# State-space section of a small vision network: a quarter of the products made with time along partitions, C spread by DMA, chunks ordered by state group first

## What is computed

```python
def _mamba(x, Win, convw, convb, Wx, Wdt, bdt, Alog, Dp, Wout):   # D_INNER 512, D_STATE 32, DT_RANK 16, D_CONV 4
    u, z = jnp.split(jnp.einsum('bld,ed->ble', x, Win), 2, axis=-1)
    ...                                                            # causal convolution of u over 4 taps
    uc = _silu(uc)
    x_dbl = jnp.einsum('bld,ed->ble', uc, Wx)
    dt = jax.nn.softplus(jnp.einsum('blr,dr->bld', x_dbl[..., :DT_RANK], Wdt) + bdt)
    Bv, Cv = x_dbl[..., DT_RANK:DT_RANK + D_STATE], x_dbl[..., DT_RANK + D_STATE:]
    A = -jnp.exp(Alog)
    def step(h, ins):
        dt_t, B_t, C_t, u_t = ins
        h = jnp.exp(dt_t[..., None] * A) * h + (dt_t * u_t)[..., None] * B_t[:, None, :]
        return h, jnp.einsum('bdn,bn->bd', h, C_t)
    ...
    y = ys.transpose(1, 0, 2) + uc * Dp
    return jnp.einsum('bld,ed->ble', y * _silu(z), Wout)
```

## Time and profile before

| | |
|---|---|
| median of 3 runs | 3977.64 us (3972.79 to 3995.63) |
| the profiled execution | 3975.0 us |
| its span, first to last instruction | 3973.3 us |
| mean granted TensorE clock | 0.942 |
| TensorE matmuls busy | 3398.2 us (86%) |
| VectorE busy | 2701.4 us (68%) |
| ScalarE busy | 2065.3 us (52%) |
| GpSimd busy | 1935.7 us (49%) |

### The profile page before, as it was taken

One profiled execution on the slowest core, in us unless ns is written; L12 is line 12 of the kernel. 1 busy time (PEld: TensorE's weight loads), 2 busy tenths in 40 slices (PEclk: granted clock), 3 DMA queues, 4 the chain that ended last, 5 costly groups with the idle time before them and its releaser, 6 DMA issues. The chain is left out here.

```text
span 3973.3 us, 59932 instructions
## 1 busy us (share of the span) xinstructions
PE 3398.2 (86%) x18880; PEld 2341.8 (59%) x18880; DVE 2701.4 (68%) x4104; ACT 2065.3 (52%) x4736; POOL 1935.7 (49%) x1912
## 2 busy tenths in 40 slices
PE   1869989989996888898888888998887889999868
PEld 0646666667654566666666666666655655555544
DVE  6442255643236999999999999999997444444441
ACT  0332223332227777787778777877774244444422
POOL 0123200000315998999999999899985000000035
PEclk9989999999997999999999999999999999989865
DMA  3068610002950000000000000000000000000035
GB/s 97 2 224 316 247 62 1 1 18 107 312 198 28 1 1 2 1 1 2 1 14 1 4 1 2 1 1 2 1 1 11 26 1 1 1 1 1 3 113 170
DMA packets 66606, 196.70 MB, mean 50 GB/s; under 512 B 12609, under 2 KB 37177, under 8 KB 55769
## 3 DMA queue, kind: packets, MB, share of 16 engines
q1 hardware_dynamic: 54936, 161.60, 11.9%
q0 software_dynamic: 11328, 30.95, 2.4%
HBM read 166.53 MB, written 25.99 MB: 48 GB/s over the span
## 5 line engine op out<-in xcount | busy, mean ns | idle before, releaser
L1905 DVE TENSOR_TENSOR_SCAN ssm_hs<-ssm_da,ssm_pb 128x512 f32<-128x512 f32 x1024 | 1236.3, 1207 | 3.6 <-ACT ssm_da L1744 3.6
L1444 POOL TENSOR_TENSOR ssm_hc<-ssm_hs,ssm_cb 128x1024 f32<-128x1024 f32 x512 | 1207.6, 2359 | 0.0
L1541 PE MATMUL ssm_py<-ssm_hc,ident 128*128 128x256 f32 x4096 | 1061.4, 382 | 2.8 <-POOL ssm_hc L1444 2.6
L1744 ACT ACTIVATE ssm_da<-ssm_dt,ssm_an 128x255 f32<-128x255 f32 x2048 | 871.7, 502 | 133.4 <-POOL ssm_dtu L1392 89.9
L1541 PEld LDWEIGHTS ssm_py<-ssm_hc,ident 128*128 128x128 f32 x4096 | 705.6, 191 | 79.6 <-POOL ssm_hc L1444 5.7
L1888 DVE TENSOR_TENSOR ssm_pb<-ssm_pb,ssm_dtu 128x512 f32<-128x512 f32 x1024 | 690.5, 674 | 29.6 <-PE ssm_pb L1527 25.8
L1527 PE MATMUL ssm_pb<-ssm_bst,ssm_eyeb 96*128 96x256 bf16 x2048 | 403.7, 279 | 208.1 <-DVE ssm_hs L1905 192.8
L1527 PEld LDWEIGHTS ssm_pb<-ssm_bst,ssm_eyeb 96*128 96x128 bf16 x2048 | 147.5, 98 | 485.3 <-DVE ssm_hs L1905 410.1
L1134 DVE TENSOR_REDUCE duo_mxr<-duo_ring 128x4 f32<-128x1024 f32 x128 | 156.7, 1225 | 200.4 <-PE duo_ring L861 189.2
L2374 PE MATMUL moe_pu<-moe_up,moe_xt 128*128 128x512 f32 x568 | 269.8, 598 | 1.8 <-ACT moe_xt L2504 1.8
L2246 POOL DMA_INDIRECT moe_xr<-moe_x_dram,moe_rowx x71 | 68.9, 971 | 345.6 <-PE ln_ps L2363 197.7
(11 more groups left out here) (590 smaller groups left out, 5791.0 us busy)
## 6 DMA issues: line engine op xcount, KB each, us to landing
moe_up<-in_moe_up SPq DMA_DIRECT2D x72, 1024.0 KB, 7.4
moe_down<-in_moe_down SPq DMA_DIRECT2D x72, 512.0 KB, 4.9
sw_wt<-in_sw_w SPq DMA_DIRECT2D x47, 192.5 KB, 2.9
moe_x_dram<-moe_tok SPq DMA_DIRECT2D x32, 128.0 KB
moe_yg<-moe_y_dram SPq DMA_DIRECT2D x16, 256.0 KB, 3.1
tok_w<-in_wd SPq DMA_DIRECT2D x4, 576.0 KB, 13.4
out<-h SPq DMA_DIRECT2D x1, 2056.0 KB, 6.3
tok_pix<-in_img SPq DMA_DIRECT2D x1, 2048.0 KB, 9.7
```

Of the source, the lines that this page charges most:

```text
L1444: nc.gpsimd.tensor_tensor(hc[:, n % 2, part_], hs[:, n % 2, part_], cb[:, q * NQ_ + 4 * half:q * NQ_ + 4 * half + 4, :], ALU.mult).then_in ...
L1541: ins = nc.tensor.matmul(py[:, j % 2, 0:L], k.ident[:], hc[:, n % 2, st, :], start=False, stop=(q == QN - 1 and st == NQ_ - 1))
L1744: ins = nc.scalar.activation(da[:, n % 2, 2 * m + o, 1:L], dt2[:, v, j, 1:L], ACT.Exp, scale=a_n[:, d, j, st:st + 1])
L1905: nc.vector.tensor_tensor_scan(two(hs[:, n % 2, 2 * m:2 * m + 2, :]), two(da[:, n % 2, 2 * m:2 * m + 2, :]), two(pb[:, p % 4]), 0.0, ALU.m ...
```

## The change

- **Order of chunks:** the group of states q is outermost, the channel block j innermost. `cb` holds two groups of eight states instead of all 32; all four blocks' sums are open at once (`sums`), and `out_chunk` runs four times at the start of the next unit.
- **C by DMA:** `spread_c` and ScalarE's 32 copies go. ScalarE copies the rows of B and C to `crow`; SyncE stores C to DRAM (`store_c`) and loads one group, spread to all partitions, at a time (`load_c`), when GpSimd has finished the group that used the buffer.
- **The last two states of each chunk (step m = 3):** dt u is turned by TensorE to time along partitions (`turn_steps`, eight 128x128 transposes a unit) and copied by ScalarE (`take_steps`). There B of one state is a column, so ScalarE makes the product of all 512 channels with a scale (`products`, two passes of 512 columns per state and group). TensorE turns it back into `pb` (`turn_products`, four transposes in place of two matmuls), and VectorE makes only 48 products a unit in place of 64.
- **Directions:** `take` goes; `project` reads `x` itself and ScalarE reads the projections backwards.
- **Places:** the work for the next unit stands two to four chunks earlier; `last_token` and `lead` now stand after chunk 0, all of `soften` before the unit begins (chunks 11 and 12). The last states are copied once a chunk.
- **Waits:** VectorE waits for `hc` once a chunk, at step 0, for both halves of chunk n - 2.

```diff
-        cb = sb("cb", [P, NS_, L])
+        cb = sb("cb", [P, 2, NQ_, L])
...
+                def store_c(u, v):
+                    sp.wait_ge(s["crow_in"], u + 1)
+                    sp.dma_start(c_dram[bass.ds(u, 1)].rearrange("o n t -> (o n) t"), crow[NS_:2 * NS_, v, :]).then_inc(s["c_out"], 16)
+
+                def load_c(u, q):
+                    if q == 0:
+                        sp.wait_ge(s["c_out"], Turn(u, 16)(16))
+                    sp.wait_ge(s["hc_done"], Turn(u, 2 * NCH, 16)(2 * DJ * (q - 1)))
+                    sp.dma_start(cb[:, q % 2], c_dram[bass.ds(u, 1), q * NQ_:(q + 1) * NQ_, 0:L].rearrange("o n t -> (o n) t").partition_broadcast(P)).then_inc(s["c_odd" if q % 2 else "c_even"], 16)
...
                     for n in range(NCH):
-                        j, q = n // QN, n % QN
+                        q, j = n // DJ, n % DJ
                         if j == 0:
-                            pool.wait_ge(s["c_free"], c_free(NQ_ * (q + 1)))
+                            pool.wait_ge(s["c_odd" if q % 2 else "c_even"], Turn(u, 32)(16 * (q // 2 + 1)))
...
-                            nc.gpsimd.tensor_copy(h_l[:, v, j, q * NQ_ + 4 * half:q * NQ_ + 4 * half + 4], hs[:, n % 2, part_, L - 1])
-                            nc.gpsimd.tensor_tensor(hc[:, n % 2, part_], hs[:, n % 2, part_], cb[:, q * NQ_ + 4 * half:q * NQ_ + 4 * half + 4, :], ALU.mult).then_inc(s["hc_done"], 1)
-                        if before is not None:
+                            if half:
+                                nc.gpsimd.tensor_copy(h_l[:, v, j, q * NQ_:(q + 1) * NQ_], hs[:, n % 2, :, L - 1])
+                            nc.gpsimd.tensor_tensor(hc[:, n % 2, part_], hs[:, n % 2, part_], cb[:, q % 2, part_, :], ALU.mult).then_inc(s["hc_done"], 1)
+                        if n == 0 and before is not None:
+                            last_token(u - 1, 1 - v, before)
+                        if n == 12:
+                            last_rate(u, v, d)
+                        if after is not None:
                             if n == 0:
-                                last_rate(u - 1, 1 - v, before)
-                            if n == 2:
-                                last_token(u - 1, 1 - v, before)
-                        if n == 0:
-                            soften(u, v, 2, 4, 8)
-                        if after is not None:
-                            if n == 1:
-                                take(u + 1, after)
-                            if n == 2:
                                 pool.wait_ge(s["dt_set"], Turn(u, DJ)(DJ))
                                 settle(pool, k)
                                 lead(1 - v)
-                            if n in (5, 6):
-                                taps(u + 1, 1 - v, n - 5)
-                            if n in (9, 10):
-                                cut(u + 1, n - 9)
+                            if n in (2, 3):
+                                taps(u + 1, 1 - v, n - 2)
+                            if n in (7, 8):
+                                cut(u + 1, n - 7)
+                            if n == 10:
+                                cut_low(u + 1, 1 - v, 0, 4, 0)
+                            if n == 11:
+                                soften(u + 1, 1 - v, 0, 2, 4)
                             if n == 12:
-                                cut_low(u + 1, 1 - v, 0, 4, 0)
-                            if n == 13:
...
+                def turn_steps(u, v, h):
+
+                    for j in range(DJ):
+                        ins = nc.tensor.transpose(pm[:, h, j * P:j * P + P], dtu2[:, v, j, h * P:h * P + P], k.ident[:])
+                    ins.then_inc(s["dtut_done"], 1)
...
+                def turn_products(u, v, p):
+
+                    q, j = p // 4 // DJ, p // 4 % DJ
+                    if j == 0:
+                        pe.wait_ge(s["tp_in"], Turn(u, QN)(q + 1))
                     pe.wait_ge(s["b_free"], Turn(u, SUB, 4)(p - 3))
                     for o in range(2):
-                        st = 2 * (p % (NS_ // 2)) + o
+                        for h in range(2):
+                            ins = nc.tensor.transpose(pb[:, p % 4, o, h * P:h * P + P], tp[:, q % 2, o, h, j * P:j * P + P], k.ident[:])
+                    ins.then_inc(s["b_done"], 1)
+
+                def spread_b(u, v, p):
+
+                    if p % 4 == TM:
+                        turn_products(u, v, p)
+                        return
+                    if p == 0:
+                        pe.wait_ge(s["stacked"], u + 1)
+                    pe.wait_ge(s["b_free"], Turn(u, SUB, 4)(p - 3))
+                    for o in range(2):
+                        st = p // 4 // DJ * NQ_ + 2 * (p % 4) + o
...
+                                if n in (1, 2) and m in (0, 2):
+                                    project(u + 1, after, 2 * (n - 1) + m // 2)
...
+                                    turn_b(u + 1, 1 - v)
+                                if n == 14 and m in (0, 2):
+                                    if m == 0:
+                                        pe.wait_ge(s["dt_set"], Turn(u + 1, DJ)(DJ))
+                                        pe.wait_ge(s["last_out"], u + 2)
+                                    turn_steps(u + 1, 1 - v, m // 2)
...
+                def take_steps(u):
+                    for h in range(2):
+                        act.wait_ge(s["dtut_done"], Turn(u, 2)(h + 1))
+                        nc.scalar.copy(dtut[:, h, :], pm[:, h, :]).then_inc(s["dtut_in"], 1)
+
+                def products(u, v, q, o, free):
+
+                    if o == 0:
+                        act.wait_ge(s["last_out"], u + 1)
+                        act.wait_ge(s["dtut_in"], Turn(u, 2)(2))
+                        if free is not None:
+                            act.wait_ge(s["b_done"], free)
+                    st = q * NQ_ + 2 * TM + o
+                    for h in range(2):
+                        ins = nc.scalar.activation(tp[:, q % 2, o, h, :], dtut[:, h, :], ACT.Copy, scale=bt[:, v, h, st:st + 1])
+                    if o:
+                        ins.then_inc(s["tp_in"], 1)
...
+                        if n // DJ + 1 < QN and n % DJ in (1, 2):
+                            q = n // DJ
+                            products(u, v, q + 1, n % DJ - 1, Turn(u, SUB)(4 * DJ * q) if q or before is not None else None)
                         if after is not None:
-                            if n == 4:
+                            if n == 1:
                                 take_u(u + 1, 1 - v, after, 0)
-                            if n == 5:
+                            if n == 2:
                                 take_u(u + 1, 1 - v, after, 1)
                                 take_u(u + 1, 1 - v, after, 2)
...
+                            if n == 14:
+                                take_steps(u + 1)
+                            if n == 15:
+                                for o in range(2):
+                                    products(u + 1, 1 - v, 0, o, Turn(u, SUB)(12 * DJ))
...
                             if p + 1 < SUB:
-                                product(u, v, p + 1)
+                                if (p + 1) % 4 != TM:
+                                    product(u, v, p + 1)
                             elif after is not None:
                                 product(u + 1, 1 - v, 0)
-                            if m % 2 == 0:
-                                dve.wait_ge(s["hc_done"], Turn(u, 2 * NCH, 4)(2 * n + m // 2 - 3))
+                            if m == 0:
+                                dve.wait_ge(s["hc_done"], Turn(u, 2 * NCH, 16)(2 * n - 2))
                             dve.wait_ge(s["da_done"], Turn(u, SUB)(p + 1))
-                            dve.wait_ge(s["b_set"], Turn(u, SUB)(p + 1))
+                            if m == TM:
+                                dve.wait_ge(s["b_done"], Turn(u, SUB)(p + 1))
+                            else:
```

250 lines of the change are left out of this document (127 added, 123 removed).

## The result

The changed kernel takes 4139.07 us (median of 4 runs, 4121.71 to 4142.69), beside 3986.64 for the kernel before (median of 4 now): a ratio of **1.0368** (95% interval 1.033 to 1.0406), some 150 us slower. The forecast, 4032 us and at most 4090, had the sign right and about a third of the size.

What follows compares the result with a forecast made beforehand. VectorE sets the pace (597 of 600 us), GpSimd follows at 91%. Work of 16 x 103.2 = 1651 us, stalls 192, start and end 11 make 1854 against 1800: +54, so 4032 us, range 3925 to 4090.

Steps and rivals of the forecast that it cites:

- Chain A: Chunks 0 to 6: `lead`, `take_u`, `project`, `total` and two `taps` make VectorE wait at chunk 6, about 6.6 us a unit.
- GpSimd's burst: Chunks 10 to 12: GpSimd carries 13.3 us of extra work against 1.5 us of spare time a chunk.
- The start: First scan waits for `soften` of blocks 2 and 3, eight transposes, copies and passes of products: some 10 us.
- A and B in 14 units at 13.0: Stalls of both chains summed: 13.0 us in 14 units, some 9.5 in the first, none in the last: 192 us.
- Chain B: Chunks 8 to 15: from `root` through `soften` and GpSimd's work, VectorE stalls 3.4 and 2.9 us, 6.4 a unit.
- delays VectorE within the same stall: Chunk 14: TensorE's wait for `dt_set` holds back B, inside VectorE's 2.9 us stall before chunk 15.
- the upper bound: GpSimd's 102.3 us, its present idle time 9.8 and new waits 3.7 and 1.4: 117.2 a unit, +86 us overall.
- No stall: Rival: VectorE stays the bound, GpSimd's backlog fits its slack; 3 to 5 us of stall a unit, 3900 us; chance 0.11.
- one chain: Rival: `lead` or the products cost less, so only one of the two chains stalls: 3937 us; chance 0.11.
- break-even: Rival: stalls of 8 to 10.5 us, chains overlapping each other's slack: within 20 us of 3978; chance 0.12.
- C was not late either: Rival: the load of C takes over 25 us, each us beyond costing 1 us in 64 groups; 4160 us; chance 0.04.
- The clock did fall: Rival: transposes do not count as activity, TensorE falls to half the clock: 5360 us; chance 0.02.

Runs made afterwards that it cites:

- lead_early: Changed kernel with GpSimd's `last_token` and `lead` moved ahead of chunk 0 instead of behind it: 4078.94 us, ratio 1.0214.
- root_split: Changed kernel with ScalarE's root of the norm moved behind chunk 10's decays and `take_dt` 2, the affine to ahead of `take_dt` 3: 4086.65 us, ratio 1.0259.
- turn_later: Changed kernel with the eight transposes of the steps and ScalarE's two copies of them moved from chunk 14 to chunk 15: 4132.78 us, ratio 1.0339.
- warm: Changed kernel with 16 extra matmuls, their result overwritten, in TensorE's gap before the wait for `dt_set` in chunk 14: 4156.58 us, ratio 1.0443.
- warm8: Changed kernel with 8 extra matmuls in TensorE's gap before the wait for `dt_set`, where warm has 16: 4136.51 us, ratio 1.0379.
- seven_moves: Changed kernel plus lead_early, root_split, turn_later, later `decay_last`, `scale`, second `taps`, time steps and `fuse`, `cut_low` on VectorE, first unit reordered: 3989.88 us, ratio 0.9959.
- all64: Changed kernel with VectorE making all 64 products again, without ScalarE's passes and the 64 transposes a unit for them: 4093.81 us, ratio 1.0266.

## Why the prediction was wrong

**Right:** the sign and its reason, that chains across engines and not VectorE's work decide the unit. *Chain A* was sized well: forecast 6.6 us a unit, measured 7.0. Of these, 4.9 stand before chunks 5 and 6; the other 2.1 stand before B in chunks 2 and 3, which the forecast had TensorE late for and did not charge. ScalarE's wait for the memset of `lead` is 3.7 us a unit (forecast 3.8). With `lead` out of the way (lead_early) 3.4 us are left, and the forecast's sum without those 3.7 leaves 2.9, the burst of the two `taps`. *GpSimd's burst* also: from its start on chunk 10 to the end of chunk 12 I had 23.2 us, and by GpSimd's timeline it is 23.3 (1822.62 to 1845.88):

```profile
1822.62 2.36 POOL L1475 TENSOR_TENSOR ssm_hc<-ssm_hs,ssm_cb 128x1024 f32<-128x1024 f32 x1 [6.04 <-PE ssm_py L1586]
...
1843.53 2.35 POOL L1475 TENSOR_TENSOR ssm_hc<-ssm_hs,ssm_cb 128x1024 f32<-128x1024 f32 x1
```

*ScalarE, the transposes at the full clock, C by DMA* cost about what was said, and the load of C is never waited for. *The start* was 9.9 us against 10.

**The first step that failed** is the sum's list of chains: "A and B in 14 units at 13.0". There is a third, M, between them, of 4.2 us: 3.3 before B in chunks 8 to 10 and 0.9 before `scale`. Chain B was followed from `root` to ScalarE's `soften` alone. On the way `take_dt` 2 stands behind `root`, eight decays and the products, and TensorE's fourth `time_step` waits for it, with B of chunk 10 and the totals behind:

```profile
1809.47 0.48 ACT L1773 ACTIVATE ln_rstd<-ln_ps,eps 128x257 f32<-128x257 f32 x1 [5.20 <-PE ln_ps L1604]
...
1810.30 3.28 ACT L1790 ACTIVATE ssm_da<-ssm_dt,ssm_an 128x255 f32<-128x255 f32 x8
...
1813.48 1.32 ACT L1812 ACTIVATE ssm_tp<-ssm_dtut,ssm_bt 128x512 f32<-128x512 f32 x2
...
1814.71 0.46 ACT L1747 ACTIVATE ssm_dt<-ln_ps,ssm_cols 128x257 f32<-128x257 f32 x1
```

ScalarE stood idle 5.2 us before `root`, waiting for `variance`. TensorE stood 2.89 us, and GpSimd, behind the totals, began its burst after 6.04 us of idle time where the forecast had 1.4. root_split took `take_dt` 2 out of this chain and got 52 us back; M fell to 2.2 us and B to 7.1.

**The second** is in chain B: TensorE's wait for `dt_set` "delays VectorE within the same stall". turn_later leaves 2.9 us for GpSimd under it, exactly the stall forecast for chunk 15; but the wait was 4.3, so 1.4 us stick out. They are TensorE's clock. (The other 0.7 of B's 8.6 against 6.4 stand before chunks 13 and 14, 4.1 us where the forecast had 3.4.) TensorE's rows behind both of its waits, the one for `take_dt` 2 and the one for `dt_set`:

```profile
1815.58 0.70 PE L1536 MATMUL ln_ps<-ssm_rank,ssm_wdt 16*128 16x257 f32 x2 [2.89 <-ACT ssm_e L1748]
1816.20 1.00 PE L1560 MATMUL ssm_pb<-ident,ssm_tp 128*128 128x128 f32 x4
1817.00 1.92 PE L1586 MATMUL ssm_py<-ssm_hc,ident 128*128 128x256 f32 x4
...
1850.35 1.11 PE L1549 MATMUL ln_ps<-ident,ssm_dtu 128*128 128x128 f32 x4 [4.79 <-POOL ssm_dtu L1422]
1851.26 1.06 PE L1560 MATMUL ssm_pb<-ident,ssm_tp 128*128 128x128 f32 x4
1852.11 1.91 PE L1586 MATMUL ssm_py<-ssm_hc,ident 128*128 128x256 f32 x4
1853.82 0.44 PE L1573 MATMUL ssm_pb<-ssm_bst,ssm_eyeb 96*128 96x256 bf16 x2
1854.09 1.03 PE L1586 MATMUL ssm_py<-ssm_hc,ident 128*128 128x256 f32 x4
```

The transposes, products and total at 1850.35 take 1.85 us more, by their durations, than the same three kinds of rows in warm at the full clock. The clock of five stretches (us, TensorE busy, granted clock):

```profile
1638.80:1642.60 3.80, 3.78 (x11) 0.55 0.00 0
1642.60:1648.00 5.40, 5.40 (x33) 1.00 0.00 0
1845.60:1850.30 4.70, 0.00 (x0) 0.50 0.00 0
1850.30:1854.00 3.70, 3.65 (x14) 0.51 0.02 4
1854.00:1860.00 6.00, 6.00 (x38) 1.00 0.01 3
```

The stretches right behind these two gaps (2.40 us before 1638.8, 4.8 before 1850.3) run near the lower of the two levels, 1.2 GHz, just where the others wait, and the next at 2.4 GHz. The clock need not have waited for the second gap to fall: from 1840.3 to 1845.6, after several shorter waits of TensorE and before this gap, it was 0.50 already. At 1850.3 it costs 15 x 1.4 = 21 us of some 150, by this sum; the medians of warm8 neither show that it comes back nor rule it out.

**The third** is the upper bound, 117.2 us a unit, "GpSimd's 102.3 plus all its idle time of now". It took GpSimd's idle time for a constant, 14.9 us a unit with the two new waits. Measured over 1400 to 2600 us GpSimd is busy 100.8 us a unit, near the forecast's 102.3, and idle 23.2. It was idle 308 us behind totals in the whole run, since a late hand-over of TensorE keeps GpSimd waiting, and then GpSimd keeps VectorE. As I read it, two buffers of `hs` let neither catch up; no run had a third. GpSimd's busy share, 81% here, bounds nothing.

**The sum.** The section took 158 us more, not 54: 104 us apart. The start (9.9 against 10) and the first unit (112.6 against 103.2 + 9.5) came as forecast. The last unit, without idle time, took 101.5 us, 2.7 less than forecast with its end. The 14 units between took 123.9 us each against 116.2: 7.7 x 14 = 108 us. Of the 7.7, idle time is 6.8 (A 0.4, M 4.2, B 2.2 over the forecast) and the rest VectorE's own time.

**The rivals.** No stall, one chain, break-even: none came, since the stalls are 19.8 us a unit in three places. C was not late either: it lands in 5.5 us. The clock did fall, from 0.99 to 0.92, but where TensorE had idle time and not because of transposes: seven_moves runs its 72 a unit at 0.97, and all64, which has only the 8 of dt u, has 0.97 as well. So the rule of the Trainium skill that the prediction weighed ("TensorE: Matmul & The Clock Gate", Part 4), in its strictest reading, does not show in these runs.

## What to carry to other kernels

When work is taken from the engine that sets the pace, list for every other engine what it waits for in each stage of the loop, and give each chain the new, shorter time: of the nearly 8 us a unit that the forecast lacked, 4 were a chain that was not on its list. A wait that is removed gives back only what lies between it and the next one in line (of 4.3 us at most 1.7 came back), while independent chains add up; so move all of them before judging the saving. The saved products, worth minus 45 us as the change stood, were worth 84 us once `lead`, `root`, `take_dt`, the `taps`, `cut_low` and some smaller pieces had been moved.

## What the hardware showed that was not expected

- Filling a gap of TensorE: 16 matmuls of fp32 with 256 columns took 8.1 us, where their 32 rows would take 6.9 at 0.216 each; the gap's low clock applied to the first rows, 0.43 us apart. In warm8, 8 matmuls took 5.2 us instead of 3.5, half of their rows at 0.43.
- A pass of 1028 columns on VectorE with both inputs in SBUF takes 1.20 us alone and up to 3.41 where it meets a GpSimd operation, of which it waits out the rest: it ends 1.08 to 1.09 us after it in 15 of 15 units.
